# The three masks of each scan chunk on ScalarE, head by head, in place of GpSimd's broadcast products

## The chip, the cores and the metric

The kernel runs on one core of one Trainium2 chip. The time is the device time of one execution in microseconds (us). Five engines work side by side, each through its own queue in order, and wait for one another on semaphores: TensorE (PE: matmuls and transposes), VectorE (DVE), ScalarE (ACT), GpSimd (POOL) and SyncE (SP, which issues the loads and stores). Here GpSimd works on SBUF alone, and PSUM is read by VectorE and ScalarE.

## The reference

One layer for 2 sequences of 512 tokens, width 512, in fp32:

```python
h = x + mamba2(rmsnorm(x, ln1_w))        # in-projection to z, xs, Bs, Cs, dt; conv of 4 taps; silu
h = h + down(silu(gate(h2)) * up(h2))    # h2 = rmsnorm(h, ln2_w), inner width 1792
x = layernorm(x + h)
x = layernorm(x + bitlinear_ffn(x))      # three ternary weights, inner width 1376
```

Inside `mamba2` the scan goes over chunks of 128 tokens with 4 heads. For one chunk, with `a = dt * A` per token and head:

```python
cs = jnp.cumsum(a, axis=-1)
Ldec = jnp.where(tri, jnp.exp(cs[..., :, None] - cs[..., None, :]), 0.0)
att = jnp.einsum('bchqn,bchkn->bchqk', Cc, Bc) * Ldec
Yd = jnp.einsum('bchqk,bchkp->bchqp', att, Xdt)          # Xdt = Xc * dt
states = jnp.einsum('bchq,bchqn,bchqp->bchpn', dec_end, Bc, Xdt)
```

## The kernel before, in words

Two sequences b, each of four chunks c, so eight chunks (b, c), numbered t = 4b + c. A tile of a chunk has 128 partitions and 512 columns, which are 4 heads of 128. Every fp32 product is made of two or three fp32r products of a high and a low part.

`build_schedule` writes out one list of steps, and each engine walks that same list in its block and takes the steps that concern it. So the place of a step in the list is its place in every engine's queue. The list goes: eight normalisations (`norm1`) and transposes (`turn1`); `inproj` (b, j), ten products per sequence (j = 0 to 5 are the channels that are convolved, 6 to 9 are z); and the scan, whose parts for sequence 0 begin at `inproj` (0, 8) and for sequence 1 at (1, 8). The second sequence's scan lies beside the first products `p1` and `p2` of the gate and up weights (`alpha`). Then come the other products of that stage (one level of Strassen's scheme), the down projection, and the ternary layer, each with a dense TensorE.

What a chunk (b, c) does, in the order of its steps:
- `until` (L719 to L738, function `up_to_query`): three masks of 128 x 512, for head h the triangle `tri` (128 x 128, bf16, ones where key <= query) times one number per partition: `until_h` and `until_l` from the high and low part of dt * A, and `dt_until` from dt. It waits for `dt_ready` (the last dt step of the sequence on VectorE), for the matmuls of the chunk before that read `until_h` and `until_l`, and, ahead of `dt_until`, for `dt_taken` (VectorE's product with the last one).
- `chunk`: TensorE transposes x and B (`xb`, L1487 and L1488), multiplies C by B (`cb`, L1491), then `strict` times `until_h` and `until_l` (`seg`, L1496 and L1497: the differences of the cumulated sums), and for c > 0 `ones` times the same (`csb`, L1501 and L1502). ScalarE copies `xb` out (`xnbn`, L960) and takes the exponentials (`decay` L964, `gend` L970, `ecs` L973).
- `decay`: VectorE multiplies `decay` by `dt_until` (L1188) and by `cb` (L1199); GpSimd makes `xs` (L792), scales `ecs` (L800) and adds the skip's diagonal (L805).
- `until` of the next chunk stands right behind `decay`, ahead of the next `inproj`. For chunk (0, 0) it stands behind `inproj` (0, 5), for chunk (1, 0) ahead of `inproj` (1, 7).
- `state`: TensorE makes the new state (`st`, L1512) and y (L1519, L1522); VectorE updates `state` (L1208 and L1213) and multiplies y by silu(z) into `yt` (L1225); ScalarE rounds it (`yt_h`, L980); VectorE makes `yt_l` (L1228).
- `outproj`: TensorE's product with the output weights (L1386 to L1391, the same lines as `inproj`); VectorE adds x (L1236); ScalarE squares and sums (L985); GpSimd adds x again (L810) and makes `rstd` (L659, L660). `norm2` (VectorE, L1246) and `turn2` (TensorE L1422, ScalarE `xT_f` L923 and `xT_h` L925, VectorE `xT_l` L1060) follow.

ScalarE also starts each convolution (L944, with a scale and a bias per partition), takes the silus (L948, L952), rounds weights (L844, L879), and sums absolute values of ternary weights (L868). The dt of a sequence takes a chain of small VectorE steps on 128 x 16 (L1143 to L1166) with an exponential (L935) and a logarithm (L937) of ScalarE in it. PSUM has eight banks, four in `psA` (for `inproj` and the gate and up products) and four in `psB` (for the scan, `outproj` and the transposes), each given out in turn by the order of the list: a job opens its bank when the job four places ahead of it has been read out.

Of the kernel before, what the change touches and what calls it, by code (L numbers as in the profile page):

```python
# [21 lines left out]
F32 = mybir.dt.float32  # L22
# [3 lines left out]
ALU = mybir.AluOpType  # L26
ACT = mybir.ActivationFunctionType

P = 128
# [269 lines left out]
def layer_kernel(nc, hidden, w_in, w_dt, conv_w, conv_b, a_log, d_skip, dt_bias, w_out, ln1_w, ln2_w,  # L299
                 w_gu, w_dn, f_gu, f_dn, out):  # L300
    with ExitStack() as ctx:
# [190 lines left out]
        def done_b(job):  # L492
            return b_done, DONE_B.index(job) + 1
# [16 lines left out]
        def heads(tile):  # L510
            return tile.rearrange("p (h q) -> p h q", h=H)

        def chunk(c):
            return slice(c * P, (c + 1) * P)
# [66 lines left out]
        def tile_of(step):  # L581

            return step[1] if len(step) == 2 else NC * step[1] + step[2]
# [63 lines left out]
        def _(pool):  # L647
# [69 lines left out]
                    nc.gpsimd.tensor_tensor(beta[:, f % 2, 1, cols], wsum[:, f % 2, cols],  # L717
                                            beta[:, f % 2, 0, cols].bitcast(F32), ALU.subtract).then_inc(gb_low, 1)

            def up_to_query(t):  # L720

                b, c = t // NC, t % NC
                pool.wait_ge(dt_ready, b + 1)
                if t >= 1:

                    last = ((t - 1) // NC, (t - 1) % NC)
                    pool.wait_ge(*done_b(("csb" if last[1] > 0 else "seg", *last)))
                for to, part in ((until_h, adt_h), (until_l, adt_l)):
                    nc.gpsimd.tensor_tensor(
                        heads(to[:]), tri[:].unsqueeze(1).to_broadcast([P, H, P]),  # L730
                        part[:, b, H * c:H * c + H].bitcast(F32).unsqueeze(2).to_broadcast([P, H, P]),
                        ALU.mult).then_inc(until_ready, 1)

                if t >= 1:
                    pool.wait_ge(dt_taken, t)
                nc.gpsimd.tensor_tensor(heads(dt_until[:]), tri[:].unsqueeze(1).to_broadcast([P, H, P]),
                                        dtT[:, b, H * c:H * c + H].unsqueeze(2).to_broadcast([P, H, P]), ALU.mult)\
                    .then_inc(dt_until_ready, 1)  # L738

            for step in SCHEDULE:  # L740
                kind, at = step[0], step[1:]
                if kind == "load" and LOADS[at[0]][0] == "out":
# [7 lines left out]
                elif kind == "load" and LOADS[at[0]][0] == "dn":  # L750

                    n = at[0]
                    pool.wait_ge(high_ready, SPLITS.index(n) + 1)
                    raw_arrived(pool, n)
                    for cols, high, low in dn_parts(LOADS[n][1]):
                        last = nc.gpsimd.tensor_tensor(low, by_tile(raw[:, n % RAW_SLOTS, cols]), high.bitcast(F32),
                                                       ALU.subtract)
                    last.then_inc(low_ready, 1)
                elif kind == "act":

                    b, f = at
                    n = FM * b + f
                    pool.wait_ge(acth_ready, n + 1)
                    high, low = act_hl[:, n % ACT_SLOTS, 0, :], act_hl[:, n % ACT_SLOTS, 1, :]
                    nc.gpsimd.tensor_tensor(low, act[:, f, b, :], high.bitcast(F32), ALU.subtract)\  # L765
                        .then_inc(actl_ready, 1)
                elif kind == "load" and LOADS[at[0]][0] == "gb":
                    weight_sums(at[0])
                elif kind == "gsplit":
                    low_parts_of_sums(at[0])  # L770
                elif kind == "norm1":
                    pool.wait_ge(sq_ready, at[0] + 1)
                    reciprocal_deviation(step, sq[:, at[0]:at[0] + 1], 1.0 / D)
                elif kind == "prepare":
                    prepare()
                elif kind == "load" and at[0] in INPROJ[IN_ON_DVE:]:
                    low_part_of_input(at[0])
                elif kind == "until":
                    up_to_query(tile_of(step))
                elif kind == "decay":  # L780
                    b, c = at
                    t = NC * b + c
                    if c < NC - 1:

                        i = (NC - 1) * b + c
                        pool.wait_ge(wend_ready, i + 1)
                        pool.wait_ge(*freed_b(("xb", b, c)))
                        if i >= 1:

                            before = (b, c - 1) if c else (b - 1, NC - 2)  # L790
                            pool.wait_ge(*done_b(("st", *before)))
                        nc.gpsimd.tensor_tensor(heads(xs[:]), xnbn[:, 0:P].unsqueeze(1).to_broadcast([P, H, P]),  # L792
                                                wend[:, t % 2, :].unsqueeze(2).to_broadcast([P, H, P]), ALU.mult)\
                            .then_inc(xs_ready, 1)
                    if c > 0:

                        i = (NC - 1) * b + c - 1
                        pool.wait_ge(*freed_b(("csb", b, c)))
                        pool.wait_ge(xbc_ready, NX * (b + 1))
                        nc.gpsimd.tensor_tensor(heads(ecs[:]), heads(ecs[:]), xbc[b][:, 2:NX, chunk(c)], ALU.mult)\  # L800
                            .then_inc(cs_scaled, 1)

                    pool.wait_ge(*freed_b(("cb", b, c)))
                    pool.wait_ge(diag_ready, 1)
                    nc.gpsimd.tensor_tensor(decay[:], decay[:], diag_d[:], ALU.add).then_inc(att_ready, 1)  # L805
                elif kind == "outproj":
                    t = tile_of(step)
                    i = NT + t
                    pool.wait_ge(*freed_b(step))
                    nc.gpsimd.tensor_tensor(x[:, t, :], x[:, t, :], nrm[:, t % 2, :], ALU.add).then_inc(u_ready, 1)  # L810
                    pool.wait_ge(sq_ready, i + 1)
                    reciprocal_deviation(step, sq[:, i:i + 1], 1.0 / D)
                elif kind in ("ln1", "ln2"):
                    t = tile_of(step)
                    i = t if kind == "ln1" else NT + t
                    pool.wait_ge(bn_ready, i + 1)
                    reciprocal_deviation(step, mv[:, i, 1:2], 1.0)
                elif kind == "inter":
                    b, f = at
                    n = FF * b + f  # L820
                    pool.wait_ge(inth_ready, n + 1)
                    pool.wait_ge(*freed_a(("fu", b, f)))
                    nc.gpsimd.tensor_tensor(int_l[:, f, :], prod_t[:, n % 2, :], int_h[:, f, :].bitcast(F32),  # L823
                                            ALU.subtract).then_inc(int_ready, 1)

        @block.scalar
        def _(s):
# [5 lines left out]
                nc.scalar.activation(aneg[:], alog_sb[:], ACT.Exp).then_inc(aexp_ready, 1)  # L833

            sums = 0

            for step in SCHEDULE:
                kind, at = step[0], step[1:]
# [67 lines left out]
                        .then_inc(sq_ready, 1)  # L906
                elif kind == "prepare":
                    prepare()
                elif kind == "thigh":

                    c = at[0]
# [770 lines left out]
```

## Time and profile before

| | |
|---|---|
| median of 3 runs | 504.51 us (504.22 to 505.97) |
| profiled execution, its own time | 506.52 us |
| its span in the trace | 504.7 us |
| busy: TensorE | 478.6 us, 95% |
| busy: VectorE | 322.3 us, 64% |
| busy: GpSimd | 273.8 us, 54% |
| busy: ScalarE | 236.7 us, 47% |

The busy time is the sum of an engine's instructions over the span. The chain that ended last is followed back from the last instruction to what released each. The granted clock of TensorE is given as a share of 2.4 GHz, so 0.50 is 1.2 GHz. Scan and in-projection lie between about 24 and 180 us of the span. In a timeline the columns are start, duration, engine, line and operation, output and inputs, and in square brackets the idle time of the engine ahead of the instruction with what ended it.

### The profile page before, as it was taken

How to read it: one execution, taken by the hardware profiler on the slowest of the kernel's cores; microseconds unless marked ns; L12 is line 12 of the kernel's file. 1: busy time of each engine (PE TensorE's matmuls, PEld its weight loads, DVE VectorE, ACT ScalarE, POOL GpSimd, SP SyncE). 2: the span in 40 equal slices, each digit the busy share in tenths (PEclk: the TensorE clock that was granted, in tenths of full speed). 3: DMA queues.
4: the chain of work that ended last, by engine and by line, in shares of the span. 5: the costliest groups of instructions: out<-in, count | busy, mean ns of one | idle time of the engine just before them, and what ended most of it. 6: DMA issues, size and time to landing. Idle time of an engine off the chain costs nothing.

```text
span 504.7 us, 6223 instructions
## 1 busy us (share of the span) xinstructions
PE 478.6 (95%) x2104; PEld 380.0 (75%) x2104; DVE 322.3 (64%) x482; ACT 236.7 (47%) x444; POOL 273.8 (54%) x278
## 2 busy tenths in 40 slices
PE   8999999979898989999999979999989999999995
PEld 8886677767576768788788757788868888888884
DVE  3785786643777856677998879994955722421233
ACT  5869767665556666455342333333905441023200
POOL 5726475443852586766877588954703432233421
PEclk9999999998999999999999989999999999999999
DMA  7522021022202415342332145330210000100002
GB/s 247 199 98 85 1 84 62 21 64 77 88 25 83 151 58 188 127 172 82 123 125 99 47 150 204 126 125 1 84 63 0 1 0 1 62 23 0 2 6 77
DMA packets 14431, 40.80 MB, mean 81 GB/s; under 512 B 2368, under 2 KB 2368, under 8 KB 14400
## 3 DMA queue, kind: packets, MB, share of 16 engines
q1 hardware_dynamic: 14400, 40.41, 23.1%
q8 instruction: 17, 0.28, 0.2%
q14 instruction: 14, 0.11, 0.1%
HBM read 38.30 MB, written 2.10 MB: 80 GB/s over the span
## 4 chain that ended last, share of the span: by engine, by line
PE 76%; DVE 9%; POOL 6%; issue 4%; ACT 3%; DMA 2%; POOLq 0%; SPq 0%; DVEq 0%; ACTq 0%
PE psA L1609 8%; PE psA L1610 8%; PE psA L1398 6%; PE psA L1400 6%; PE psB L1619 4%; PE psB L1618 4%; PE psA L1404 3%; PE psA L1406 3%; PE psA L1584 3%; PE psA L1588 3%; PE psA L1587 3%; DVE xbc L1175 2%; PE psA L1386 2%; PE psA L1391 2%; PE psA L1387 2%
## 5 line engine op out<-in xcount | busy, mean ns | idle before, releaser
L1609 PE MATMUL psA<-xT_h,q_gu 128*128 128x512 f32 x176 | 70.2, 399 | 1.5 <-DVE x L1330 1.5
L1610 PE MATMUL psA<-xT_l,q_gu 128*128 128x512 f32 x176 | 69.1, 393 | 0.0
L823 POOL TENSOR_TENSOR int_l<-prod_t,int_h 128x512 fp32r<-128x512 f32 x22 | 28.5, 1297 | 59.3 <-ACT int_h L1043 59.2
L1350 DVE TENSOR_TENSOR prod_t<-gate_t,psA 128x512 f32<-128x512 f32 x22 | 15.2, 689 | 54.5 <-PE psA L1610 49.4
L717 POOL TENSOR_TENSOR beta<-wsum,beta 128x512 fp32r<-128x512 f32 x28 | 36.0, 1308 | 25.5 <-ACT beta L899 25.5
L1038 ACT ACTIVATE gate_t<-psA 128x512 f32<-128x512 f32 x22 | 13.1, 597 | 76.9 <-PE psA L1610 76.9
L765 POOL TENSOR_TENSOR act_hl<-act,act_hl 128x512 fp32r<-128x512 f32 x28 | 42.2, 1527 | 9.1 <-ACT act_hl L1017 9.1
L1609 PEld LDWEIGHTS psA<-xT_h,q_gu 128*128 128x128 f32 x176 | 33.1, 188 | 10.1 <-issue 2.0
L1319 DVE SCALAR_TENSOR_TENSOR q<-raw,scl,qtmp 128x512 fp8e4<-128x512 f32 x33 | 39.8, 1205 | 1.2
L1610 PEld LDWEIGHTS psA<-xT_l,q_gu 128*128 128x128 f32 x176 | 33.1, 188 | 7.3
L1317 DVE TENSOR_SCALAR qtmp<-raw,scl 128x512 bf16<-128x512 f32 x33 | 33.2, 1005 | 3.1 <-DMA raw<-in_f_gu_t 3.1
L1618 PE MATMUL psB<-q_dn,int_h 128*128 128x512 f32 x88 | 34.3, 389 | 0.0
L1619 PE MATMUL psB<-q_dn,int_l 128*128 128x512 f32 x88 | 34.3, 389 | 0.0
L1386 PE MATMUL psA<-xT_h,win_h 128*128 128x512 f32 x80 | 32.7, 408 | 1.2 <-DVE xbc L1175 1.2
L1007 ACT ACTIVATE c<-c 128x512 f32<-128x512 f32 x14 | 8.9, 633 | 50.3 <-DVE c L1270 50.3
L1387 PE MATMUL psA<-xT_l,win_h 128*128 128x512 f32 x80 | 31.4, 392 | 0.0
L659 POOL TENSOR_SCALAR var<-mv 128x1 f32<-128x1 f32 x16 | 4.7, 295 | 42.6 <-DVE mv L1067 42.2
L1175 DVE SCALAR_TENSOR_TENSOR xbc<-psA,convw_sb,xbc 128x511 f32<-128x511 f32 (+2 forms) x36 | 26.8, 746 | 0.8
L1017 ACT ACTIVATE act_hl<-act 128x512 fp32r<-128x512 f32 x28 | 16.9, 623 | 17.8 <-PE psB L1588 12.4
L1357 DVE SCALAR_TENSOR_TENSOR x<-psB,scl,x 128x512 f32<-128x512 f32 x8 | 6.0, 751 | 26.6 <-PE psB L1619 26.6
L1398 PE MATMUL psA<-xT_h,beta 128*128 128x512 f32 x56 | 22.4, 399 | 0.3 <-DVE act L1286 0.3
L810 POOL TENSOR_TENSOR x<-x,nrm 128x512 f32<-128x512 f32 x8 | 12.0, 1499 | 19.1 <-DVE nrm L1236 19.1
(251 smaller groups left out, 1391.6 us busy)
## 6 DMA issues: line engine op xcount, KB each, us to landing
raw<-in_f_gu_t SPq DMA_DIRECT2D x22, 512.0 KB, 3.4
raw<-in_w_gu_t SPq DMA_DIRECT2D x14, 512.0 KB, 3.8
raw<-in_f_dn_t SPq DMA_DIRECT2D x10, 512.0 KB, 3.2
raw<-in_w_gu_t SPq DMA_DIRECT2D x14, 256.0 KB, 2.7
raw<-in_w_dn_t SPq DMA_DIRECT2D x7, 512.0 KB, 3.3
raw<-in_w_in_t SPq DMA_DIRECT2D x5, 512.0 KB, 4.3
x<-in_hidden SPq DMA_DIRECT2D x8, 256.0 KB, 5.4
out<-x SPq DMA_DIRECT2D x8, 256.0 KB, 2.0
```

Of the source, the lines that this page charges most:

```text
L717: nc.gpsimd.tensor_tensor(beta[:, f % 2, 1, cols], wsum[:, f % 2, cols], beta[:, f % 2, 0, cols].bitcast(F32), ALU.subtract).then_inc(gb_l ...
L765: nc.gpsimd.tensor_tensor(low, act[:, f, b, :], high.bitcast(F32), ALU.subtract)\
L1175: add = nc.vector.scalar_tensor_tensor(out=xbc[b][:, j, back:L], in0=bank_a(job)[:, 0:L - back], scalar=convw_sb[:, j, TAPS - 1 - back:TAP ...
L1317: link(nc.vector.tensor_scalar(qtmp[:, cols], raw[:, n % RAW_SLOTS, cols], scl[:, 9 + w:10 + w], None, ALU.is_lt))
L1319: last = nc.vector.scalar_tensor_tensor(out=q8[:, f, cols], in0=raw[:, n % RAW_SLOTS, cols], scalar=scl[:, 6 + w:7 + w], in1=qtmp[:, cols] ...
L1386: nc.tensor.matmul(ps, sh, mh, start=i == 0, stop=False)
L1387: nc.tensor.matmul(ps, sh, ml, start=False, stop=False)
L1398: nc.tensor.matmul(ps, weights[:, 0, chunk(k)], high[:, k, :], start=opens and k == 0, stop=False, skip_group_check=not opens)
L1609: nc.tensor.matmul(ps, w, seq(xT_h, k, b), start=k == 0, stop=False)
L1610: done = nc.tensor.matmul(ps, w, seq(xT_l, k, b), start=False, stop=k == KD - 1)
L1618: nc.tensor.matmul(ps, int_h[:, f, chunk(c)], q_dn[:, f, :], start=f == 0, stop=False)
L1619: done = nc.tensor.matmul(ps, int_l[:, f, chunk(c)], q_dn[:, f, :], start=False, stop=f == FF - 1)
```

## The change

The step `until` leaves GpSimd's walk through the list and enters ScalarE's, at the same places. Each of the three products over 4 heads, with `tri` and the number broadcast by strides, becomes four activations (`Copy`) of 128 x 128 with the number as a scale per partition; the semaphore is raised by the last of four. The waits are the same, and one on `consts_ready` is added. Nothing else differs.

```diff
--- before.py
+++ after.py
@@ -717,26 +717,6 @@
                     nc.gpsimd.tensor_tensor(beta[:, f % 2, 1, cols], wsum[:, f % 2, cols],
                                             beta[:, f % 2, 0, cols].bitcast(F32), ALU.subtract).then_inc(gb_low, 1)
 
-            def up_to_query(t):
-
-                b, c = t // NC, t % NC
-                pool.wait_ge(dt_ready, b + 1)
-                if t >= 1:
-
-                    last = ((t - 1) // NC, (t - 1) % NC)
-                    pool.wait_ge(*done_b(("csb" if last[1] > 0 else "seg", *last)))
-                for to, part in ((until_h, adt_h), (until_l, adt_l)):
-                    nc.gpsimd.tensor_tensor(
-                        heads(to[:]), tri[:].unsqueeze(1).to_broadcast([P, H, P]),
-                        part[:, b, H * c:H * c + H].bitcast(F32).unsqueeze(2).to_broadcast([P, H, P]),
-                        ALU.mult).then_inc(until_ready, 1)
-
-                if t >= 1:
-                    pool.wait_ge(dt_taken, t)
-                nc.gpsimd.tensor_tensor(heads(dt_until[:]), tri[:].unsqueeze(1).to_broadcast([P, H, P]),
-                                        dtT[:, b, H * c:H * c + H].unsqueeze(2).to_broadcast([P, H, P]), ALU.mult)\
-                    .then_inc(dt_until_ready, 1)
-
             for step in SCHEDULE:
                 kind, at = step[0], step[1:]
                 if kind == "load" and LOADS[at[0]][0] == "out":
@@ -775,8 +755,6 @@
                     prepare()
                 elif kind == "load" and at[0] in INPROJ[IN_ON_DVE:]:
                     low_part_of_input(at[0])
-                elif kind == "until":
-                    up_to_query(tile_of(step))
                 elif kind == "decay":
                     b, c = at
                     t = NC * b + c
@@ -834,6 +812,28 @@
 
             sums = 0
 
+            def up_to_query(t):
+
+                b, c = t // NC, t % NC
+                s.wait_ge(dt_ready, b + 1)
+                s.wait_ge(consts_ready, 1)
+                if t >= 1:
+
+                    last = ((t - 1) // NC, (t - 1) % NC)
+                    s.wait_ge(*done_b(("csb" if last[1] > 0 else "seg", *last)))
+                for to, part in ((until_h, adt_h), (until_l, adt_l)):
+                    for h in range(H):
+                        masked = nc.scalar.activation(to[:, chunk(h)], tri[:], ACT.Copy,
+                                                      scale=part[:, b, H * c + h:H * c + h + 1].bitcast(F32))
+                    masked.then_inc(until_ready, 1)
+
+                if t >= 1:
+                    s.wait_ge(dt_taken, t)
+                for h in range(H):
+                    masked = nc.scalar.activation(dt_until[:, chunk(h)], tri[:], ACT.Copy,
+                                                  scale=dtT[:, b, H * c + h:H * c + h + 1])
+                masked.then_inc(dt_until_ready, 1)
+
             for step in SCHEDULE:
                 kind, at = step[0], step[1:]
                 if kind == "load" and LOADS[at[0]][0] in ("in", "out"):
@@ -906,6 +906,8 @@
                         .then_inc(sq_ready, 1)
                 elif kind == "prepare":
                     prepare()
+                elif kind == "until":
+                    up_to_query(tile_of(step))
                 elif kind == "thigh":
 
                     c = at[0]
```

## Rows read from the trace of the kernel before

**Rows 1.** The page: busy time of each engine; the chain that ended last.

```profile
PE 478.6 (95%) x2104; PEld 380.0 (75%) x2104; DVE 322.3 (64%) x482; ACT 236.7 (47%) x444; POOL 273.8 (54%) x278
...
PE 76%; DVE 9%; POOL 6%; issue 4%; ACT 3%; DMA 2%; POOLq 0%; SPq 0%; DVEq 0%; ACTq 0%
```

**Rows 2.** TensorE's waits, whole span: total, times, longest.

```profile
PE psB L1386 <- DVE decay L1199: 3.1, 2, 1.6
PE psA L1398 <- DVE xT_l L1060: 2.5, 1, 2.5
```

**Rows 3.** GpSimd by line: busy us, mean ns, idle before, releaser.

```profile
L729 POOL TENSOR_TENSOR until_h<-tri,adt_h 128x512 fp32r<-128x512 bf16 x8 | 9.4, 1177 | 9.8 <-DVE adt_l L1166 9.8
L736 POOL TENSOR_TENSOR dt_until<-tri,dtT 128x512 f32<-128x512 bf16 x8 | 8.3, 1040 | 0.0
```

**Rows 4.** ScalarE by line.

```profile
L868 ACT ACTIVATE raw<-raw 128x512 f32<-128x512 f32 x33 | 20.3, 619 | 0.0
...
L944 ACT ACTIVATE xbc<-psA,convb_sb,convw_sb 128x512 f32<-128x512 f32 x12 | 9.2, 764 | 2.2 <-PE psA L1391 2.2
...
L998 ACT ACTIVATE act<-psA 128x512 f32<-128x512 f32 x11 | 6.5, 595 | 2.9 <-PE psA L1406 2.9
...
L964 ACT ACT_TABLE_LOAD x5 | 6.4, 1283 | 0.1
...
L915 ACT ACTIVATE xT_h<-t_f 128x256 fp32r<-128x256 f32 x4 | 1.7, 418 | 2.8 <-DVE t_f L1089 2.8
```

**Rows 5.** Timeline of ScalarE, 40 to 54 us.

```profile
40.21 0.62 ACT L952 ACTIVATE xbc<-xbc 128x512 f32<-128x512 f32 x1
...
44.10 0.64 ACT L952 ACTIVATE xbc<-xbc 128x512 f32<-128x512 f32 x1
...
45.78 0.59 ACT L930 ACTIVATE nrm<-psA 8x512 f32<-8x512 f32 x1 [0.55 <-PE psA L1462]
...
50.12 0.60 ACT L948 ACTIVATE sz<-psA 128x512 f32<-128x512 f32 x1 [0.28 <-PE psA L1391]
...
53.56 0.22 ACT L937 ACTIVATE dtw<-dtw 128x16 f32<-128x16 f32 x1
53.68 0.76 ACT L944 ACTIVATE xbc<-psA,convb_sb,convw_sb 128x512 f32<-128x512 f32 x1
```

**Rows 6.** Timeline of VectorE.

```profile
37.69 0.17 DVE L1166 TENSOR_TENSOR adt_l<-adt,adt_h 128x16 fp32r<-128x16 f32 x1
...
52.91 0.96 DVE L1154 SCALAR_TENSOR_TENSOR dtw<-dtw 128x16 f32<-128x16 f32 x1
...
80.92 1.12 DVE L1213 SCALAR_TENSOR_TENSOR state<-state,gend,psB 128x128 f32<-128x128 f32 x4
...
133.43 0.75 DVE L1246 SCALAR_TENSOR_TENSOR nrm<-nrm,rstd,ln_sb 128x512 f32<-128x512 f32 x1 [2.10 <-POOL rstd L660]
```

**Rows 7.** Timeline of TensorE.

```profile
45.58 0.27 PE L1487 MATMUL psB<-ident,xbc 128*128 128x128 f32 x1
...
57.09 0.47 PE L1496 MATMUL psB<-until_h,strict 128*128 128x512 f32 x1 [0.88 <-DVE state L1208]
...
83.15 0.80 PE L1496 MATMUL psB<-until_h,strict 128*128 128x512 f32 x1
```

**Rows 8.** Timeline of ScalarE, 70 to 77 us.

```profile
70.02 0.63 ACT L980 ACTIVATE yt_h<-yt 128x512 fp32r<-128x512 f32 x1 [2.50 <-DVE yt L1225]
...
76.86 0.59 ACT L925 ACTIVATE xT_h<-psB 128x512 fp32r<-128x512 f32 x1
```

**Rows 9.** Timeline of ScalarE, 103 to 111 us.

```profile
103.08 0.63 ACT L985 ACTIVATE yt_h<-nrm 128x512 fp32r<-128x512 f32 x1 [2.42 <-DVE nrm L1236]
...
110.73 0.60 ACT L925 ACTIVATE xT_h<-psB 128x512 fp32r<-128x512 f32 x1
```

**Rows 10.** Windows: length, busy PE, PEld, DVE, ACT, POOL; PEclk; DMA.

```profile
111.00:125.00 14.00, 12.57 (x43) 8.87 (x44) 6.28 (x10) 7.12 (x15) 5.96 (x7) 0.88 0.18 58
...
137.00:150.00 13.00, 13.00 (x51) 9.62 (x50) 10.30 (x16) 6.18 (x15) 8.42 (x9) 0.87 0.17 64
```

## The prediction

> **What bounds the kernel now.** I read the page first. TensorE is busy for 478.6 of 504.7 us and holds 76% of the chain that ended last, against 6% for GpSimd and 3% for ScalarE [rows 1]. The reader is to see that GpSimd's 54% costs nothing by itself: work taken from it pays only where TensorE waits for it in the end. Next come TensorE's waits [rows 2]. In the scan (about 40 to 180 us) the long ones name VectorE: `xT_l` 2.5 us once and `decay` 3.1 us in two waits. None there names GpSimd. Third, ScalarE's timeline through the scan, since the masks go there. It has few gaps: from the start of the silu at 40.21 to the bias step at 53.68 it waits 0.55 us once and 0.28 us once [rows 5]. What ScalarE makes late there goes on through VectorE to a PSUM bank or an operand that TensorE waits for.
>
> **What goes.** GpSimd loses three 128x512 products for each of eight chunks: `until_h` 1.18 us and `dt_until` 1.04 us [rows 3], `until_l` as the latter, 9.4 + 8.3 + 8.3 = 26 us in all, 3.1 us a chunk at their starts' distance.
>
> **What comes.** ScalarE gets 4 heads x 3 masks = 12 activations of 128x128 a chunk, 96 in all. None of that form is in the trace, so I bound it. 128x512 takes 619 ns and 128x256 takes 418 ns [rows 4]: 0.79 ns a column, so 128 columns take 418 - 100 = 318 ns. A following instruction starts some 100 ns before the end of the one ahead (53.56 + 0.22 against 53.68, rows 5), so 0.21 us each is the low end, if a scale per partition were free. It is not likely to be: L944, with a scale and a bias per partition, takes 764 ns where L998 takes 595 ns for the same size from PSUM [rows 4], 169 ns for two pointers. With half of it for the one pointer a mask takes 0.30 us; with all of it 0.38 us. I take 0.30 us, because two operands of one kind should share the price. A chunk is then 3.6 us of ScalarE (ends 2.5 and 4.6), all eight 29 us. I add no table load: the copies of L868 and L915 have none of their own, where the exponentials of L964 have one of 1283 ns [rows 4]. The waits moved with the masks are mostly met: the last dt step of sequence 0 starts at 37.69 [rows 6], ahead of 40.21, and eight masks (2.4 us) cover VectorE's product that frees `dt_until`.
>
> I carry 3.6 us through ScalarE's queue at each of the eight places.
>
> **(a) Chunks (0,0) and (0,1).** The first set stands between the bias step of `inproj(0,5)` and the silu at 40.21. Everything behind it moves by 3.6 us, among it the silu at 44.10 that completes `xbc`: it ends at 48.3 instead of 44.7. TensorE's transposes of the chunk wait for it and started at 45.58 [rows 7], so they stand 2.8 us. ScalarE takes up its own wait before 45.78, 0.55 us and the 0.1 us of overlap [rows 5]. The second set comes right behind the exponential of that chunk, ahead of the silu for z, the two table loads and the exponential and logarithm of sequence 1's dt. So the logarithm at 53.56 moves by 7.2 us less those 0.67 and the 0.28 us before 50.12 [rows 5]: +6.25. VectorE's dt steps wait for it. There a gain enters: steps of 16 columns took 0.96 us under GpSimd's masks (52.91, rows 6) where one of sequence 0 takes 0.17 us (37.69). Two of them stand between the exponential and the step that takes the logarithm, and a third is stretched less: without that VectorE is ready ahead of the logarithm, where it is late by an estimated 1.25 us now (three steps stretched by 0.8, 0.8 and 0.4 us, less the 0.75 us that it had in hand). `adt_l` is then 6.25 - 1.25 = +5.0 us late, the `state` copy behind it too, and TensorE's `seg` at 57.09, which already waits 0.88 us for that copy's bank [rows 7], comes at 62.1: **+5.0**, of which the 2.8 above is a part.
>
> **(b) Chunks (0,2) and (0,3).** The set of (0,2) is mostly taken up by ScalarE's waits, the last of them 2.50 us before 70.02 [rows 8]; it leaves the `yt_h` copy 0.7 us late and TensorE 0.4. The set of (0,3) stands ahead of the bias step of `inproj(1,3)` and the turn copies behind it. The `xT_h` copy at 76.86 [rows 8] ends 4.3 us later (3.6 + 0.7), at 81.7. VectorE then does in order `xT_l` 0.6, the residual sum 0.6, three convolution steps 2.3 and the state update (80.92, rows 6) from 85.2 to 86.4. TensorE's `seg(0,3)`, at 83.15 before [rows 7], needs the bank that this update frees, so it comes at 86.4; the matmul behind it needs the bank of the `yt` product, and 3.0 us of this stay: **+3.0**, the 0.4 in it.
>
> **(c) Chunks (1,0) and (1,1).** The set of (1,0) pushes a ScalarE stretch that has 2.42 us of waiting before 103.08 [rows 9] and smaller ones; by the order of the steps 0.95 us comes out behind. The set of (1,1) stands ahead of the z copy and the two turn copies whose last one is at 110.73 [rows 9]. ScalarE is full there, VectorE's `xT_l` follows it at once, and TensorE already waits 2.54 us for that (2.5 in rows 2). So all of it shows: 0.95 + 3.6 = **+4.55**.
>
> **(d) Chunks (1,2) and (1,3).** Here GpSimd was late: its sums stood behind its masks, and VectorE waited 2.10 us for `rstd` at 133.43 [rows 6]. This goes. But ScalarE's `alpha` copy for a later step comes 2 us late in its stead, VectorE's state update behind it too, and TensorE's output product, which waits for the `decay` product [rows 2], comes an estimated 0.9 us later: **+0.9**.
>
> Behind the scan nothing gives this back: TensorE's waits after 180 us are single ones under 3 us, none of which ends on a mask.
>
> **The clock.** TensorE's granted clock is 0.88 over 111 to 125 us and 0.87 over 137 to 150 [rows 10]: one fall to half (1.2 GHz) for 3.4 us in each, right behind idle times of 2.5 us and of 1.6 us. Each cost some 1.7 us of TensorE (12% of 14, 13% of 13). The change makes new idle times of 2.8, 2.9 and 3 us in (a) and (b). A fall behind the first is spent in the wait of the second; I count one of the others, **+1.7**, and keep none and two for the range.
>
> Sum: 5.0 + 3.0 + 4.55 + 0.9 + 1.7 = 15.15 us. The profiled execution has a span of 504.7 and a time of 506.52, so 1.8 us lie around the span and don't change; it is 2.0 above the median of 504.51. Against the median: 504.5 + 15.15, **519.7 us**.
>
> **A rule of the Trainium skill, weighed.** VectorE's short steps in (a) are stretched while GpSimd works (0.96 us in rows 6). Of this the Trainium skill, GPSIMD Engine Reference, "1. Specifications", says that GpSimd shares its SBUF interfaces with VectorE, and contends with VectorE instructions in a two-port mode or with two SBUF inputs. The trace agrees; by that rule alone the removal of GpSimd's 26 us would be a gain, which is rival 2 below. The Trainium skill, ScalarE: Activation LUTs, "What ACT_TABLE_LOAD costs", adds some 93 ns for each per-partition pointer: 0.30 us a mask by its figures, so the sum would stay as it is.
>
> **Rivals.**
> 1. The pointer is free: 0.21 us a mask, 2.5 us a chunk. Then (a) is 2.8, (b) 1.6, (c) 2.5, (d) nothing, no fall of the clock: +6.9, 511.4 us. For it: the logarithm on 128x16 takes only 0.22 us, so there is little fixed cost [rows 5]. Against it: 764 against 595 ns.
> 2. The relief of GpSimd decides. Place: the chain `x`, `rstd`, normalisation, `decay` at 124 to 136 us and the stretched dt steps. It gives 1.55 us (half of the 3.1 in rows 2) and 1.25 us at (a), if ScalarE's queue costs TensorE nothing: 504.5 - 2.8 = 501.7. It decides only if a set costs less than ScalarE's waits, that is under some 0.5 us in (a), a sixth of the price above. Against it: the fully used ScalarE in (a) and (c).
> 3. Gains and losses meet: ScalarE's delays run into slack that I haven't seen, 504.5 and within 0.5%. For it: ScalarE has waits in the scan (0.55, 2.50 and 2.42 us in rows 5, 8 and 9). Against it: in (a) and (c) they lie elsewhere than the late steps.
> 4. The masks cost 0.38 us: 4.6 us a chunk. (a) 7.0, (b) 4.6, (c) 6.6, (d) 2.9, and two falls 3.4: +24.5, 529 us.
> 5. The change isn't the plain exchange that it says: a copy with a scale operand needs a table that the exponential's or silu's isn't. Each set then brings a load of 1.28 us [rows 4], and ScalarE's eight cost about as much as rival 4: 529 us again.
>
> **Chances.** The forecast (mechanism and size, 515 to 524): 0.65. Rival 1: 0.15. Rival 4: 0.11. Rival 5: 0.02. Rival 2: 0.03. Rival 3: 0.04. Range 510.0 to 525.0: it takes in rival 1 and reaches toward rival 4. I count a change within 0.5% (2.5 us) as none, since the runs shown differ by 1.8 us among themselves. Faster 0.03, same 0.04, slower 0.93.
>
> **What would show it.** In the profile after: 96 activations of 128x128, near 0.40 us each and 0.30 apart; ScalarE busy for 237 + 38, about 270 us, GpSimd for 248. TensorE waits that are new: about 3 us before the first chunk's transposes (for the silu), 3 us before `seg(0,1)`, 3 us before `seg(0,3)`, and about 6 us instead of 2.5 before the first product with `alpha`. Four instead of two falls of the clock up to 180 us, or three. The stretched dt steps of sequence 1 back at 0.2 us. And all stages behind the scan as long as before. It is wrong if TensorE reaches the first `alpha` product less than 8 us late, or if a mask is under 0.25 us.

## The result and the profile after

The changed kernel takes 520.17 us (median of 4 runs, 519.0 to 520.65), the one before 504.61 us on the same chip (4 runs, 504.22 to 505.97): the ratio is 1.030, 95% interval 1.0274 to 1.0326. Forecast were 519.7 us, in a range of 510 to 525. The profiled execution took 520.4 us with a span of 518.1; the one of before took 506.52 with 504.7. So the traces differ by 13.4 us in the span and 13.9 in the time, the medians by 15.6: the profiled execution of before lies 2 us above its median, and what follows accounts for the 13.4.

The page of the changed kernel, to be read against [rows 1]:

```profile
PE 480.0 (93%) x2104; PEld 380.8 (74%) x2104; DVE 316.4 (61%) x482; ACT 263.6 (51%) x540; POOL 248.0 (48%) x254
...
PE 69%; ACT 13%; DVE 10%; issue 4%; POOL 2%; DMA 1%; POOLq 0%; SPq 0%; DVEq 0%; ACTq 0%
```

GpSimd lost 25.8 us of busy time and ScalarE gained 26.9. The share of TensorE in the chain that ended last fell from 76% to 69%, ScalarE's rose from 3% to 13%. The masks themselves, by line on ScalarE (busy us, mean ns of one, idle before):

```profile
L826 ACT ACTIVATE until_l<-tri,adt_l 128x128 fp32r<-128x128 bf16 x32 | 10.1, 390 | 0.0
L833 ACT ACTIVATE dt_until<-tri,dtT 128x128 f32<-128x128 bf16 x32 | 10.1, 390 | 0.0
L826 ACT ACTIVATE until_h<-tri,adt_h 128x128 fp32r<-128x128 bf16 x32 | 10.1, 389 | 0.0
```

They take 390 ns each and start 0.29 us apart, so a set takes 3.5 us. ScalarE's busy time is 27 and not 37 us more (96 times 0.39) because successive instructions overlap. TensorE's waits in the changed kernel, 36 to 190 us (total, times, longest), to be read against [rows 2]:

```profile
PE psA L1400 <- DVE xT_l L1062: 7.5, 1, 7.5
PE psB L1388 <- DVE decay L1201: 3.3, 2, 1.7
PE psB L1498 <- DVE state L1215: 3.1, 2, 2.2
PE psB L1489 <- ACT xbc L954: 2.6, 1, 2.6
PE psB L1498 <- DVE state L1210: 2.3, 1, 2.3
```

The four waits that the prediction named are all there: for the silu ahead of the first chunk (2.6), `seg(0,1)` (2.3), `seg(0,3)` (2.2) and the first `alpha` product (7.5 in place of 2.5). Their places on TensorE's timeline, with [rows 7]:

```profile
48.48 0.48 PE L1489 MATMUL psB<-ident,xbc 128*128 128x128 f32 x1 [2.56 <-ACT xbc L954]
...
62.90 0.47 PE L1498 MATMUL psB<-until_h,strict 128*128 128x512 f32 x1 [2.25 <-DVE state L1210]
```

```profile
91.95 0.47 PE L1498 MATMUL psB<-until_h,strict 128*128 128x512 f32 x1 [2.22 <-DVE state L1215]
```

The table has the shift of TensorE against the trace of before at these and other instructions, in us. It is read at the start of the same matmul in both traces, and it is cumulative.

| kernel | seg(0,1) | seg(0,2) | seg(0,3) | first alpha | seg(1,2) | seg(1,3) | first beta |
|---|---|---|---|---|---|---|---|
| before, start | 57.09 | 69.77 | 83.15 | 112.42 | 129.84 | 146.96 | 180.37 |
| changed | +5.8 | +6.05 | +8.8 | +14.2 | +15.3 | +13.2 | +13.2 |
| only (0,0), (0,1) | +5.3 | +5.3 | +5.35 | +5.35 | +3.7 | +3.1 | +2.9 |
| only (0,2), (0,3) | -0.5 | -0.2 | +2.5 | +2.7 | +2.6 | +2.7 | +2.55 |
| only (1,0), (1,1) | -0.2 | -0.2 | -0.2 | +4.1 | +5.1 | +4.5 | +4.3 |
| only (1,2), (1,3) | -0.1 | -0.1 | -0.1 | -0.1 | +0.9 | -1.1 | -1.1 |
| one mask set for all | -0.7 | -0.6 | -0.6 | -1.4 | -2.1 | -3.9 | -3.9 |
| constant scale | +2.0 | +3.5 | +4.95 | +7.2 | +8.5 | +6.5 | +6.5 |
| four sets moved | +2.4 | +3.8 | +3.6 | +4.7 | +5.8 | +3.8 | +3.8 |
| three sets, placed | -1.1 | -1.2 | -1.15 | -1.2 | -0.1 | -2.1 | -2.1 |

Behind the first beta product (180 us of before) nothing more is gained or lost by the changed kernel: 13.2 there and 13.4 at the end. The other kernels of the table end within 0.6 us of their shift at that product.

### The profile page after: what moved, and what is told of

Its sections match the earlier page's. It is cut to its first block, busy times and chain, and to the rows that moved or that the text cites. A ratio compares the mean times of both kernels' runs of the same rounds, so it can differ in the third digit from the quotient of the medians.

```text
span 518.1 us, 6296 instructions
## 1 busy us (share of the span) xinstructions
PE 480.0 (93%) x2104; PEld 380.8 (74%) x2104; DVE 316.4 (61%) x482; ACT 263.6 (51%) x540; POOL 248.0 (48%) x254
## 4 chain that ended last, share of the span: by engine, by line
PE 69%; ACT 13%; DVE 10%; issue 4%; POOL 2%; DMA 1%; POOLq 0%; SPq 0%; DVEq 0%; ACTq 0%
PE psA L1611 8%; PE psA L1612 8%; PE psA L1400 6%; PE psA L1402 6%; PE psB L1621 4%; PE psB L1620 4%; PE psA L1406 3%; PE psA L1408 3%; PE psA L1586 2%; PE psA L1590 2%; PE psA L1589 2%; DVE xbc L1177 2%; PE psA L1436 2%; PE psB L1400 2%; PE psB L1402 2%
## 5 line engine op out<-in xcount | busy, mean ns | idle before, releaser
L1319 DVE TENSOR_SCALAR qtmp<-raw,scl 128x512 bf16<-128x512 f32 x33 | 32.0, 970 | 2.9 <-DMA raw<-in_f_gu_t 2.9
L770 POOL TENSOR_TENSOR xs<-xnbn,wend 128x512 f32<-128x512 f32 x6 | 6.2, 1040 | 46.5 <-DVE wend L1197 46.5
L1062 DVE TENSOR_TENSOR xT_l<-psB,xT_h 128x512 fp32r<-128x512 f32 x20 | 13.4, 685 | 23.8 <-ACT xT_h L927 23.6
L1019 ACT ACTIVATE act_hl<-act 128x512 fp32r<-128x512 f32 x28 | 17.0, 623 | 18.5 <-PE psB L1590 13.2
L1400 PE MATMUL psA<-xT_h,alpha 128*128 128x512 f32 x44 | 18.6, 423 | 7.9 <-DVE xT_l L1062 7.5
```

The costliest lines, as they stand in the source:

```text
L1400: nc.tensor.matmul(ps, weights[:, 0, chunk(k)], high[:, k, :], start=opens and k == 0, stop=False, skip_group_check=not opens)
```

## The experiments

A time is compared with that of the kernel before on the same chip, as a ratio with its interval. The theory is that a set on ScalarE costs TensorE what it makes late in ScalarE's own queue ("queue theory"); the rivals are that the relief of GpSimd counts for much, that every set costs alike, or that the amount of work sets the time.

**The relief alone.** GpSimd makes the masks of the first chunk, and the other seven chunks use them.

```diff
-                elif kind == "until":
+                elif kind == "until" and tile_of(step) == 0:
...
-                    pe.wait_ge(until_ready, 2 * (NC * b + c + 1))
+                    pe.wait_ge(until_ready, 2)
...
-                    v.wait_ge(dt_until_ready, t + 1)
+                    v.wait_ge(dt_until_ready, 1)
```

> The kernel before, with the masks of the first chunk alone; the seven later chunks use those, so 21 of 24 mask products are made by no engine (the outputs of the scan are other numbers). It shows what the relief of GpSimd is worth with nothing put in its place. Queue theory (what the change costs is ScalarE's sets in front of late steps; the relief is small): 1.25 us at the dt steps of sequence 1 and up to 2 us at chunks (1,2) and (1,3), so 501 to 503 us. Contention rival (GpSimd's products slow VectorE throughout): 26 us of GpSimd gone give more than 4 us, under 500. No-relief rival: 504.5.

Measured: 502.18 us against 506.45, ratio 0.991 (0.9897 to 0.9928), so 4.4 us less. That is more than the queue theory gave (1.5 to 3.5 less) and meets the contention rival's "more than 4 us": the relief was underestimated. The trace splits it. At `seg(0,1)` it is the dt chain of VectorE (timeline; [rows 6] has the step at 52.91 with 0.96 us):

```profile
51.46 1.00 DVE L1148 SCALAR_TENSOR_TENSOR dtw<-dtw 128x16 f32<-128x16 f32 x1
...
53.06 0.18 DVE L1154 SCALAR_TENSOR_TENSOR dtw<-dtw 128x16 f32<-128x16 f32 x1
...
55.50 0.17 DVE L1166 TENSOR_TENSOR adt_l<-adt,adt_h 128x16 fp32r<-128x16 f32 x1
```

Of the dt steps one (51.46) is still stretched, beside GpSimd's `xs` and `decay`; those that stood beside the masks are back at 0.18. Then 0.7 us more come up to the first alpha product and 2.5 us from there to `seg(1,3)`. In that last stretch this kernel has one fall of the clock less than the one before (a fall is a stretch at half the granted clock), and a part of the 2.5 us is that; how much is worked out under (d) below. VectorE's busy time falls by 4.4 us (322.3 to 317.9), so it is slowed beside GpSimd, but TensorE gains only at the places named.

**The price of the pointer.** The scale per partition becomes a constant.

```diff
-                                                      scale=part[:, b, H * c + h:H * c + h + 1].bitcast(F32))
+                                                      scale=-0.01)
...
-                                                  scale=dtT[:, b, H * c + h:H * c + h + 1])
+                                                  scale=0.5)
```

> The changed kernel with a constant as scale in each of the 96 activations in place of the number per partition (so the masks hold other numbers; all else is as in the changed kernel). Queue theory with the pointer's price: a mask goes from 0.29 to about 0.20 us, a set from 3.5 to 2.4 us, and the time falls by 1.1 us for each of some four to five sets that show (two at chunks (0,0) and (0,1), one at (0,3), one at (1,1)): 513 to 516 us. Rival, that the count of instructions or the waits set it: 519 to 520.5.

The same groups by line with the constant:

```profile
L826 ACT ACTIVATE until_l<-tri 128x128 fp32r<-128x128 bf16 x32 | 7.2, 296 | 0.0
L826 ACT ACTIVATE until_h<-tri 128x128 fp32r<-128x128 bf16 x32 | 7.2, 297 | 0.0
L833 ACT ACTIVATE dt_until<-tri 128x128 f32<-128x128 bf16 x32 | 7.2, 296 | 0.0
```

One pointer costs 390 - 296 = 94 ns, and a mask is 0.20 us behind the next. The time is 512.23 us against 506.45, ratio 1.011 (1.0098 to 1.0127): 5.7 us over the kernel before, where the changed kernel is 15, so 9 to 10 us less, and the time is below the expected 513 to 516. The traces have less: 6.7 us at the first beta product and 7.1 in the span (518.1 against 511.0). On the chip of this run all 11 executions of the kernel before had a mean clock of 0.987 or 0.988 and a median of 506.45, which makes the difference to it small. At most 1.7 us of the 6.7 are the clock (10.2 us at half up to 190 us against 13.6), and the 5 us that are left fit the four or five sets of 1.1 us that were expected to show.

**Two chunks at a time.** ScalarE makes two sets and GpSimd the other six (both functions are kept):

```diff
+ON_ACT = (0, 1)          # then (2, 3), (4, 5), (6, 7)
...
-                elif kind == "until":                                  # GpSimd's walk
+                elif kind == "until" and tile_of(step) not in ON_ACT:
...
+                elif kind == "until" and tile_of(step) in ON_ACT:      # ScalarE's walk
+                    up_to_query(tile_of(step))
```

> ScalarE makes the masks of chunks (0,0) and (0,1) alone, GpSimd those of the other six. Queue theory: the loss of this place stands by itself, 5.6 us up to the second seg by the trace of the changed kernel, so 509.5 to 510.5 us. Rival, that each set costs alike (15.6 us over eight sets): 3.9 us, 508.4. The dt steps of sequence 1 should not be stretched here, since GpSimd makes no masks beside them until chunk (0,2).

> ScalarE makes the masks of chunks (0,2) and (0,3) alone. Queue theory: TensorE's seg of chunk (0,3) waits for the bank of the state update and comes 3 us later, the scan may give back a part of it later: 506.5 to 507.6 us. Rival, each set alike: 3.9 us, 508.4.

> ScalarE makes the masks of chunks (1,0) and (1,1) alone, GpSimd the rest. Queue theory: the wait of TensorE before the first alpha product grows from 2.5 to some 7 us: 4.5 to 5.4 us, 509 to 510 us. Rival, each set alike: 3.9 us, 508.4.

> ScalarE makes the masks of chunks (1,2) and (1,3) alone. The prediction had +0.9 us here; the trace of the changed kernel shows 1.0 us won between the first alpha product and the first beta product. By that trace: 502.5 to 504 us, faster than before. By the prediction's step: 505.4. Rival, each set alike: 508.4.

| sets on ScalarE | this | before beside it | ratio | interval |
|---|---|---|---|---|
| (0,0), (0,1) | 509.57 | 506.45 | 1.007 | 1.0052 to 1.0088 |
| (0,2), (0,3) | 509.22 | 504.83 | 1.0084 | 1.0054 to 1.0114 |
| (1,0), (1,1) | 510.60 | 506.45 | 1.0083 | 1.0066 to 1.01 |
| (1,2), (1,3) | 504.95 | 504.83 | 0.999 | 0.9972 to 1.0009 |

The rival of equal shares falls with the last row: the same 24 activations cost 3.5 to 4.2 us at three places and nothing that can be measured at the fourth. In the table of shifts each place's queue cost stands where the prediction put it: +5.3, +2.7 to 3, +4.1 at the first alpha, and +1.0 at `seg(1,2)`. The medians don't follow those sizes well, though (3.5, 4.2, 4.2 by the ratios). (0,2), (0,3) is above its expected 506.5 to 507.6, (1,0), (1,1) somewhat above 509 to 510, and (1,2), (1,3) missed the expected 502.5 to 504, where the prediction's 505.4 was nearer. The clock stands between: of the 17 executions of before beside (0,2), (0,3), eight had a mean clock of 0.987 or 0.988 (median 506.4) and eight had 0.991 or 0.992 (median 504.3). The four with these sets had 0.984 to 0.987; against the slower eight they are 2.8 us longer, as expected.

**GpSimd keeps its load.** The changed kernel, with GpSimd making the masks too, into a tile `again` that nobody reads:

```diff
+                    link(nc.gpsimd.tensor_tensor(
+                        heads(again[:]), tri[:].unsqueeze(1).to_broadcast([P, H, P]),
+                        part[:, b, H * c:H * c + H].bitcast(F32).unsqueeze(2).to_broadcast([P, H, P]),
+                        ALU.mult))
...
```

> The changed kernel, with GpSimd making the same masks once more into a tile that nobody reads, at their old places (one after the other by a semaphore). It takes the relief of GpSimd away and leaves ScalarE's sets. Queue theory: the 1.25 us at the dt steps and the 1 to 2 us at chunks (1,2) and (1,3) are lost again: 522 to 524 us. Rival, that the relief plays no part: 520.2.

521.16 us against 504.83, ratio 1.032 (1.0287 to 1.0345). The changed kernel beside another set of runs has 1.0292 (1.0267 to 1.0316), so the difference of some 1 us is not settled by the times, and the time is below the expected 522 to 524. On two points its trace is clear. First, GpSimd's second set runs from 54.24 to 57.5 us, and VectorE's dt steps behind the exponential follow from 57.95 at 0.17 us each: they come so late by ScalarE's queue that GpSimd's masks no longer stand beside them. So the gain of 1.25 us that (a) counts comes with the delay and not with the relief of GpSimd. Second, up to 190 us its falls of the clock are those of the second profile of the changed kernel (table below), so these two traces can be set side by side: it is 1.0 us later at the first beta product (195.86 against 194.90), and from `seg(1,2)` to `seg(1,3)` it takes 16.06 us against 15.10. There the relief of GpSimd is worth 1.0 us.

**TensorE kept busy through the long wait.** Transposes of the identity into the bank of the first alpha product, which overwrites them:

```diff
                     if f == 0:
+                        ps = open_a(("al", 0))
+                        for _ in range(100):       # then 60
+                            nc.tensor.transpose(ps[:, 0:P], ident[:], ident[:])
                         for c in range(NC):
                             pe.wait_ge(*freed_b(("turn2", 0, c)))
```

> The changed kernel with 100 transposes of the identity by TensorE into the bank of the first alpha product, ahead of its wait for xT_l (overwritten by that product). They fill the 7.5 us idle time. If the fall of the granted clock behind that idle time (6.8 us at half) costs what its length says: 3.4 us less, 516.5 to 517.5 us. Rival, that TensorE isn't what bounds that stretch, or that the clock falls for another reason: 519.5 to 520.5.

100 transposes: 521.12 us against 504.83, ratio 1.032 (1.0283 to 1.035), nothing won and above the expected 516.5 to 517.5. They took 10.9 us, and the alpha product began at 128.27 where its operand was there at 124.75.

> The changed kernel once more, on the chip of the three runs beside it, so that they are compared with it: 3.0% above the kernel before, 519 to 521 us.

> As warm_alpha, with 60 transposes in place of 100. There the 100 took 10.9 us (0.109 us each) and ended 3.4 us behind the xT_l that the alpha product waits for (128.27 against 124.75 us), so the fall of the clock that they spared was lost again in waiting for them. 60 take 6.6 us of the 7.5 us wait. If the falls of the clock cost what their length says, 3.4 us less than the changed kernel: 516 to 517.5 us. If not: within 1 us of it.

On one chip, with 505.88 us for the kernel before: the changed kernel again 520.90 (1.0292, interval 1.0267 to 1.0316), with 60 transposes 517.82 (1.0239, 1.0213 to 1.0264). So 3.1 us come back. Not all of it is shown to be the transposes' doing. They begin at 117.34, and this trace is already 1.6 us ahead of the changed kernel's at `seg(1,0)` (113.25 against 114.84 and, in the second profile, 114.99): the fall that those have at 48.2 or 60.9 is missing here. From the first alpha to the first beta product it takes 65.4 us against 67.0 and 68.2, so 1.6 to 2.8 us come with the clock that stays up behind the wait. The wait that is left for `xT_l` in that kernel, and the others as they were:

```profile
PE psB L1498 <- DVE state L1215: 3.1, 2, 2.2
PE psB L1498 <- DVE state L1210: 2.9, 1, 2.9
PE psB L1489 <- ACT xbc L954: 2.6, 1, 2.6
PE psA L1388 <- DVE xbc L1177: 1.1, 1, 1.1
PE psB L1424 <- DVE nrm L1248: 1.0, 1, 1.0
PE psA L1400 <- DVE xT_l L1062: 1.0, 1, 1.0
```

**The same work at other places.** All eight sets on ScalarE, four of them behind what they made late:

```diff
+ON_ACT = (0, 1, 2, 3, 4, 5, 6, 7)
+BEHIND = {("inproj", 0, 8): 0, ("dtturn", 1): 1, ("turn2", 0, 0): 3, ("load", 14): 5}
...
+                if step in BEHIND:                # at the end of ScalarE's step
+                    up_to_query(BEHIND[step])
```

> All 96 activations on ScalarE as in the changed kernel, but four of the eight sets stand at another place of ScalarE's queue, behind what its set made late: that of chunk (0,0) behind the z copy of inproj(0,8), that of (0,1) behind the logarithm of sequence 1's dt, that of (0,3) behind the turn copies of chunk (0,0), that of (1,1) behind the second alpha copy. ScalarE's work is the same 540 instructions. Queue theory (the place decides): most of the loss goes, 505 to 509 us. Rival, that the amount of ScalarE's work or the form of the masks sets it: above 515 us.

510.15 us against 505.88, ratio 1.0088 (1.0064 to 1.0111), above the expected 505 to 509, on a chip where the kernel before takes 1.3 us more; of the 15.0 us of the changed kernel beside it 4.3 are left. The busy times on its page:

```profile
PE 476.5 (94%) x2104; PEld 378.2 (74%) x2104; DVE 317.2 (62%) x482; ACT 262.7 (52%) x540; POOL 248.6 (49%) x254
```

ScalarE does the same 540 instructions for 262.7 us. Up to 190 us its trace has one fall of 3.4 us, against 13.6 and 17.0 us in the two profiles of the changed kernel, so up to 5.1 to 6.8 of the 10.7 us won can be the clock; the rest is the places alone. This decides against the amount of work. What is left is in TensorE's waits: 4.0 us before the first alpha product (2.5 before), and 2.2 us for `until_l` itself, which comes late at (0,0) and (0,1) now.

**A version from this.** Only the sets whose relief paid, at a place where ScalarE waits:

```diff
+ON_ACT = (1, 6, 7)
+BEHIND = {("dtturn", 1): 1}
```

> GpSimd makes the masks of chunks (0,0), (0,2), (0,3), (1,0) and (1,1) as before. ScalarE makes that of (0,1) behind the logarithm of sequence 1's dt, where it waits 3 us for VectorE, and those of (1,2) and (1,3) at their old places. Queue theory: the stretched dt steps cost 1.25 us less, chunks (1,2) and (1,3) give 0 to 1 us: 502.5 to 504.3 us, up to 2 us faster than before. Rival, that nothing is to be had from this step: 504.5 to 505.

503.81 us against 505.88, ratio 0.996 (0.9944 to 0.9975): faster than the kernel before by 0.25 to 0.56%. A part of that is the clock: against the four of the 12 executions of before that had a mean clock of 0.990 or 0.991 (median 504.6) it wins 0.8 us, against the eight with 0.987 or 0.988 (median 506.1) 2.3 us. VectorE's dt steps and ScalarE's masks beside them (timelines of this kernel; the `yt_h` copy had 3.1 us of waiting ahead of it before):

```profile
52.30 0.17 DVE L1182 SCALAR_TENSOR_TENSOR dtw<-dtw 128x16 f32<-128x16 f32 x1
...
54.73 0.17 DVE L1194 TENSOR_TENSOR adt_l<-adt,adt_h 128x16 fp32r<-128x16 f32 x1
54.82 0.68 DVE L1236 COPY state<-psB 128x512 f32<-128x512 f32 x1
```

```profile
53.37 0.21 ACT L963 ACTIVATE dtw<-dtw 128x16 f32<-128x16 f32 x1
53.49 1.26 ACT L850 ACTIVATE until_h<-tri,adt_h 128x128 fp32r<-128x128 bf16 x4
54.66 1.26 ACT L850 ACTIVATE until_l<-tri,adt_l 128x128 fp32r<-128x128 bf16 x4
55.83 1.27 ACT L857 ACTIVATE dt_until<-tri,dtT 128x128 f32<-128x128 bf16 x4
...
57.66 0.61 ACT L1006 ACTIVATE yt_h<-yt 128x512 fp32r<-128x512 f32 x1
```

`adt_l` comes at 54.73 where it came at 56.16, and TensorE is 1.1 us ahead at `seg(0,1)` and stays so up to the first alpha product. From `seg(1,2)` to `seg(1,3)` it gains 2.0 us more, on which see (d) below.

## Why the prediction came out, step by step

**Price of a mask: right.** 0.30 us apart were taken, 0.29 measured; the half of L944's 169 ns, 85 ns, against 94 measured. Rival 1 (pointer free) was built as the kernel with the constant: +6.9 predicted, +5.7 measured and +6.3 in the span. Rivals 4 and 5 are out: a mask takes 0.29 us, and ScalarE has 17 table loads in both kernels.

**(a) +5.0: right in its mechanism, with one piece missing.** The logarithm on ScalarE moved from 53.56 to 60.62, by 7.06 and not 6.25. `adt_l` on VectorE is 5.8 us late, and the gain of 1.25 us at the dt steps is there: from the logarithm's start it follows after 1.36 us, before after 2.6. In ScalarE's timeline of the changed kernel, with [rows 5]:

```profile
47.81 0.62 ACT L954 ACTIVATE xbc<-xbc 128x512 f32<-128x512 f32 x1
...
51.77 0.60 ACT L966 ACTIVATE decay<-psB 128x512 f32<-128x512 f32 x1 [0.83 <-PE psB L1499]
52.27 1.26 ACT L826 ACTIVATE until_h<-tri,adt_h 128x128 fp32r<-128x128 bf16 x4
...
60.62 0.21 ACT L939 ACTIVATE dtw<-dtw 128x16 f32<-128x16 f32 x1
```

The 0.83 us ahead of the exponential at 51.77 are the piece. TensorE was at half its clock from 48.2 to 51.6, from the end of the 2.6 us wait on, so `seg` ended late and ScalarE's queue with it. "A fall behind the first is spent in the wait of the second" was wrong. With a fall there the shift at `seg(0,1)` is +5.8, or +5.3 with these sets alone, whose fall came at 47.7. In the second profile of the changed kernel no fall came before 60.9: the exponential (50.48) has no wait ahead of it, the logarithm is at 59.33, and the shift is +4.5. So the step was 0.5 us too large without a fall and 0.3 to 0.8 too small with one. The 1.25 us are there for another reason than given, as the kernel with GpSimd's load kept shows.

**(b) +3.0: right.** +3.0 from `seg(0,1)` to `seg(0,3)`, +3.0 from -0.5 to +2.5 with these sets alone.

**(c) +4.55: right up to the clock.** +4.3 from `seg(0,3)` to the first alpha product with these sets alone; +5.4 in the changed kernel, where a fall from 92.6 to 96.0 lies between, and +4.5 in its second profile, which has none there. The wait for `xT_l` is 7.5 us; about 6 was forecast.

**(d) +0.9: the sign was wrong.** The queue cost is there: +1.0 from the first alpha product to `seg(1,2)` with these sets alone, +1.1 in the changed kernel, and +0.5 is left at the output product (136.97 against 136.46). Then both give back what they lost and more: 2.0 us from `seg(1,2)` to `seg(1,3)`. The wait before the output product was not shorter (1.57 us before, 1.72 now), but the fall of the clock behind it at 137.0 didn't come. The windows of the kernel with only these two sets show it, with [rows 10] (PEclk is the third column from the end):

```profile
111.00:125.00 14.00, 12.68 (x44) 9.13 (x45) 6.34 (x10) 8.27 (x21) 6.00 (x6) 0.88 0.17 59
...
137.00:150.00 13.00, 13.00 (x57) 9.74 (x58) 10.19 (x18) 9.67 (x26) 6.69 (x7) 1.00 0.18 67
```

From the output product to the transposes of chunk (1,3) TensorE takes 8.21 us where it took 9.81 with the fall. But the clock alone doesn't bring this to the end. The kernels with only (0,0), (0,1) and only (1,0), (1,1) leave the masks of (1,2) and (1,3) to GpSimd, and they have no fall there either:

| kernel | masks of (1,2), (1,3) | fall there | seg(1,2) to seg(1,3) |
|---|---|---|---|
| before; only (0,2), (0,3) | GpSimd | yes | 17.12; 17.14 |
| only (0,0), (0,1); only (1,0), (1,1) | GpSimd | no | 16.50; 16.50 |
| GpSimd keeps its load | both | no | 16.06 |
| changed; only (1,2), (1,3) | ScalarE | no | 15.08; 15.08 |

So the missing fall is worth 0.6 us while GpSimd makes the masks, and taking them from it is worth 1.4 us more. The reason is in VectorE's steps ahead of the `state` update whose bank `seg(1,3)` needs. The same step in two timelines, first with GpSimd at work (only (0,0), (0,1); its sum `x`, behind its masks, runs from 146.87 to 148.32), then behind it (only (1,2), (1,3); there `x` ends at 142.56), and TensorE's wait in the former:

```profile
147.11 1.76 DVE L1137 TENSOR_TENSOR alpha<-raw,alpha 128x512 fp32r<-128x512 f32 x1
```

```profile
143.43 0.68 DVE L1137 TENSOR_TENSOR alpha<-raw,alpha 128x512 fp32r<-128x512 f32 x1
```

```profile
150.05 0.47 PE L1521 MATMUL psB<-until_h,strict 128*128 128x512 f32 x1 [0.40 <-DVE state L1238]
```

That is the failed step: the prediction counted the relief of GpSimd here for the wait for `rstd` only, and kept both old falls and counted new ones on top. Whether the masks' place has to do with the fall's absence is open; it is absent with GpSimd's masks too.

**The clock, +1.7: the sum fits, the parts don't.** Granted clock at half, by start and length in us, up to 190 us:

| kernel | falls | in all |
|---|---|---|
| before | 113.1 3.4; 137.0 3.4 | 6.8 |
| changed | 48.2 3.4; 92.6 3.4; 123.3 6.8 | 13.6 |
| changed, profiled again | 60.9 6.8; 122.3 10.2 | 17.0 |
| only (0,0), (0,1) | 47.7 3.4 | 3.4 |
| only (0,2), (0,3) | 115.1 3.4; 139.0 3.4 | 6.8 |
| only (1,0), (1,1) | 112.0 10.2 | 10.2 |
| only (1,2), (1,3) | 112.4 3.4 | 3.4 |
| one mask set for all | 110.5 3.4 | 3.4 |
| constant scale | 60.0 3.4; 118.0 6.8 | 10.2 |
| GpSimd keeps its load | 60.9 6.8; 122.3 10.2 | 17.0 |
| 60 transposes | 90.7 3.4 | 3.4 |
| four sets moved | 117.7 3.4 | 3.4 |
| three sets, placed | 112.3 3.4 | 3.4 |

6.8 us more at half are at most 3.4 us of time; 1.7 were counted. In all: 5.0 + 3.0 + 4.55 + 0.9 + 1.7 = 15.15 stand against 13.4 in the first pair of traces (14.4 with the second profile of the changed kernel). The shifts of the four kernels at the first beta product add up to 8.65 us (2.9 + 2.55 + 4.3 - 1.1), against 13.2 for all sets together; by the ratios of the runs it is 11.4 against 15. With half of the falls' length taken off (6.8 less 3.4 for the changed kernel), the shift at the first beta product is 9.8; the four parts give 4.6 + 2.55 + 2.6 + 0.6 = 10.35 in the same way. So by this bookkeeping the places' costs add and the clock doesn't. It is not shown, because a fall beside a wait costs less than half its length: of the 6.8 us from 123.3 on, 3.3 lie inside the wait that ends at 126.59, and without the fall at 137.0 TensorE is 1.6 us earlier at the transposes of (1,3) and, where GpSimd makes the masks, only 0.6 at `seg(1,3)`.

**Rival 2, the relief: underestimated.** 2.8 us were given, 4.4 measured with the masks of seven chunks gone. It lost by size, as said, but the part of it at the dt steps (1.25 forecast; the kernel without later masks goes from +0.6 at `seg(0,0)` to -0.7 at `seg(0,1)`) can be had by a set in a gap of ScalarE, which the last kernel shows.

**Luck.** 519.7 against 520.17 is closer than the working deserves. The terms give 1.75 us more than the first pair of traces does, and the median of before lies 2 us under its profiled execution, which offsets it. That gap is most likely a fall of the clock itself. Among the 40 further executions of before, 27 had a mean clock of 0.987 or 0.988, and 12 had 0.990 to 0.992; on one chip with eight of each the medians are 506.4 and 504.3 us, and 3.4 us at half are 1.7 of 504 us, 0.0034 of the mean clock. The profiled execution has 0.987. So the forecast added a sum worked out from the one kind to a median of the other.

## What to carry to other kernels

Work moved to an engine with an idle share of half can cost a good half of its time (15 of 28 us here) if each piece stands in the queue ahead of something that is late already; read the timeline of the receiving engine at each place, and put the piece behind the late step, into the gap that the trace shows. A fall of TensorE's clock can come or go from one execution to the next (up to 2 us here), so count existing falls as things that may go, and compare several runs with their mean clocks, and not single traces, where less than 2 us matter. What a missing fall gives back depends on who is late next: look for a kernel that lacks the fall alone before giving it the credit. Moving only the pieces whose relief shows on the path made this a gain of 0.4%.

## What was not expected of the hardware

- The scale per partition costs 94 ns in each 128x128 activation here, with an fp32r and with an fp32 output: a third of the 0.29 us from one mask to the next.
- Two profiles of the one changed kernel had the clock at half for 13.6 and 17.0 us, and at different places. Up to 190 us the falls last 3.4 us or two or three times that in every trace here.
- An idle time of 1.57 us had a fall behind it in two kernels (before, and only (0,2), (0,3)) and the same 1.57 us before the same matmul had none in two others (only (0,0), (0,1) and only (1,0), (1,1)). What decides was not tried.
- A VectorE sum of two 128x512 operands took 1.76 us while GpSimd ran a sum of 128x512 and 0.68 us when no such work ran on it; steps on 128x16 took 0.96 and 0.17 us.
- The transposes of 128x128 that filled the wait took 0.109 us each at the full clock, so 100 of them overran a wait of 7.5 us.
